# A convolution-attention hybrid on one core: causal attention by transposed scores, with six images in one schedule

## What is computed

```python
# 1. attention over channels: 8 heads of 24 channels, 24x24 logits per head
x = x + w_proj @ (softmax(norm(q) @ norm(k).T * temperature) @ v) + b_proj
# 2. causal attention over tokens: 6 heads of 32, 1024 x 1024 scores per head
t = layer_norm(tokens(x)); q, k, v = t @ Wq, t @ Wk, t @ Wv
att = softmax(where(causal, q @ k.T / sqrt(192), -inf)); x = x + att @ v
# 3. feed-forward, binarized weights, activations quantized by the
#    largest magnitude over a group of 6 images (5 groups, the last 2 images give 0)
x = x + quant(gelu(quant(layer_norm(x) @ sign(W1).T + b1)) @ sign(W2).T + b2)
```

## Time and profile before

| | |
|---|---|
| median of three executions | 4890.53 us |
| profiled execution, its span | 4894.14 us, 4892.3 us |
| TensorE busy (matmul), mean granted clock | 4119.3 us (84%), 0.948 |
| VectorE busy | 3418.6 us (70%) |
| ScalarE busy | 2759.7 us (56%) |
| GpSimd busy | 359.1 us (7%) |
| DMA, mean of 16 engines | 13.3% |

### The profile page before, as it was taken

How to read it: one execution, slowest core, us unless ns; L and a number is a source line. 1 busy time by engine, 2 the same in 40 slices (tenths; PEclk the granted TensorE clock), 3 DMA queues, 4 the chain that set the end, 5 groups by cost and what they waited for, 6 DMA issues and landing times.

```text
span 4892.3 us, 114220 instructions
## 1 busy us (share of the span) xinstructions
PE 4119.3 (84%) x38848; PEld 2965.8 (61%) x38848; DVE 3418.6 (70%) x6624; ACT 2759.7 (56%) x5791; POOL 359.1 (7%) x311
## 2 busy tenths in 40 slices
PE   3989897879898878989887879889878989887878
PEld 2766664566676636766664566666536667664565
DVE  3767677777676667767677777676677767676776
ACT  1555555646565555555555655555565555565655
POOL 0000002000000120000002000000120000002000
PEclk8999998999999989999998999999989999998999
DMA  2111111011121101111111011121101111111011
GB/s 60 40 34 34 34 40 27 0 47 34 34 54 40 34 0 39 34 34 34 35 40 27 0 47 34 41 53 34 34 0 40 34 34 34 40 34 27 0 40 40
DMA packets 46377, 161.59 MB, mean 33 GB/s; under 512 B 10098, under 2 KB 10612, under 8 KB 45684
## 3 DMA queue, kind: packets, MB, share of 16 engines
q1 hardware_dynamic: 45812, 154.38, 13.3%
HBM read 28.52 MB, written 25.17 MB: 11 GB/s over the span
## 4 chain that ended last, share of the span: by engine, by line
issue 76%; PE 13%; POOL 6%; DVE 2%; ACT 2%; DMA 0%; POOLq 0%; SPq 0%; ACTq 0%; DVEq 0%
PE S L685 5%; PE PT L754 4%; POOL hi_z L478 2%; POOL hi_z L497 1%; POOL rstd L473 1%; POOL rstd L493 1%; ACT work L908 1%; POOL NK L468 1%; PE PT L649 1%; PE OUT L669 1%; DVE work L364 0%; DVE nmax L1103 0%; DMA B<-in_b 0%; PE S L635 0%; PE S L693 0%
## 5 line engine op out<-in xcount | busy, mean ns | idle before, releaser
L863 ACT ACTIVATE work<-S,nmax 128x256 f32<-128x256 f32 (+7 forms) x1536 | 1141.4, 744 | 1113.6 <-DVE nmax L1103 1048.5
L1103 DVE TENSOR_REDUCE nmax<-S 128x1 f32<-128x256 f32 (+7 forms) x1536 | 1157.4, 754 | 845.8 <-PE S L637 830.0
L649 PE MATMUL PT<-ident,work 128*128 128x128 f32 x6912 | 1112.7, 281 | 214.2 <-DVE work L364 184.4
L649 PEld LDWEIGHTS PT<-ident,work 128*128 128x128 f32 x6912 | 748.0, 142 | 430.5 <-DVE work L364 260.4
L364 DVE COPY work<-PT 128x512 f32<-128x512 f32 (+3 forms) x1536 | 893.5, 583 | 57.4 <-PE PT L649 52.3
L685 PE MATMUL S<-odd,W1b 128*128 (+1 forms) x2160 | 567.2, 419 | 96.0 <-ACT work L908 47.0
L685 PEld LDWEIGHTS S<-odd,W1b 128*128 128x128 f16 x2160 | 215.2, 106 | 419.8 <-issue 148.6
L635 PE MATMUL S<-KS,QS 128*128 128x512 f16 (+3 forms) x1152 | 333.1, 345 | 105.7 <-issue 57.0
L867 ACT ACTIVATE work<-PT 128x512 f32<-128x512 f32 (+3 forms) x768 | 331.8, 432 | 53.4 <-PE PT L649 53.4
L637 PE MATMUL S<-causal,identb 128*128 128x128 bf16 x1536 | 342.4, 223 | 0.0
L635 PE MATMUL S<-odd 128*128 128x512 f16 (+3 forms) x1152 | 315.1, 328 | 16.9 <-ACT work L863 14.8
(11 more groups left out here) (183 smaller groups left out, 5760.9 us busy)
## 6 DMA issues: line engine op xcount, KB each, us to landing
X<-in_x SPq DMA_DIRECT2D x32, 768.0 KB, 5.4
odd<-hi_z SPq DMA_DIRECT2D x128, 192.0 KB, 4.3
odd<-odd SPq DMA_DIRECT2D x128, 192.0 KB, 4.3
out_y<-work SPq DMA_DIRECT2D x64, 384.0 KB, 3.7
QS<-hi_z SPq DMA_DIRECT2D x64, 192.0 KB, 3.7
QS<-odd SPq DMA_DIRECT2D x64, 192.0 KB, 4.2
KS<-hi_z SPq DMA_DIRECT2D x64, 192.0 KB, 4.7
KS<-odd SPq DMA_DIRECT2D x64, 192.0 KB, 4.6
```

The source lines that it names most:

```text
L649: last = tr(bank[:, P * (j - c0):P * (j - c0) + P], PS[m % 2][:, m // 2 % 2, P * j:P * j + P], ident[:, :])
L863: A(PS[n % 2][:, n // 2 % 2, 0:w], S[:, n % 2, 0:w], ACT.Exp, bias=nmax[:, n % MAXES:n % MAXES + 1], accum_out=rowsum[:, sum_col(n):sum_co ...
L1103: v.tensor_reduce(nmax[:, n % MAXES:n % MAXES + 1], S[:, n % 2, 0:P * (qtile(n) + 1)], AX.X, ALU.max, negate=True).then_inc(max_made, 1)
```

## The change

Attention no longer turns the exponentials. It makes the scores twice.

A first pass (`score_block`, `max_block`) makes them with queries on partitions, as before, only to take the row maxima: 72 blocks of up to 512 keys an image, in two banks (`SM`). `split_rows` cuts the negated maxima into three bfloat16 parts, `turn_rows` turns them with matmuls, and ScalarE copies them into `MR`, where a row belongs to a head and a part.

A second pass (`turned_block`) makes them with keys on partitions: 72 blocks of 128 keys by up to 512 queries, in three banks (`ST`). A second matmul adds the negated maxima to every row (`SEL` picks the head's three rows of `MR`), and a third adds the mask where a block touches the diagonal. ScalarE takes the exponential of a block, without bias and without row sum, into a ring of 12 buffers (`PX`). `weigh` multiplies a set of four (or two) blocks with V, in four groups of 32 array columns, with up to 512 queries moving. GpSimd adds up the blocks of a head (`presum`), 66 instructions an image, and TensorE sums over the keys with 16 matmuls of one column per accumulated group (kind "s"), VectorE takes the reciprocals, and the result of a group is turned back (kind "b") and added (`add_to_t1`).

One image is 72 ticks. The maxima of an image are taken 40 ticks ahead of its turned blocks (`LEAD`). The three rounds of the pair loop become one unrolled stretch of 432 ticks and 8 more; at its end the first 40 maxima blocks of the next group's first image and the front of it are done too. The last two images have a stretch of their own. The front's steps stand at new ticks, from 38 before to 30 behind tick 0 of the image that precedes theirs. The layer norm's normalising moves from VectorE to GpSimd (8 instructions an image), its rounding from VectorE to ScalarE (2). The front has two banks of its own. TensorE waits for all 16 stacking DMAs before the first block of an image. The tail is the same.

```diff
+TICKS = 72
+LEAD = 40
+RING = 12
...
+def make_blocks():
+    out = [(c, h, c, j, h) for c in range(2) for j in range(4 * c + 4) for h in range(4)]
+    out += [(2, h, c, j, h - 4 + 2 * c) for j in range(8) for c in ((1, 0) if j < 4 else (1,)) for h in (4, 5)]
+    return out
...
+def width(i):
+    return 512 - max(0, P * BLOCKS[i][3] - 512 * BLOCKS[i][2])
...
+def pv_tick(k):
+    return set_blocks(k)[-1] + (5 if SETS[k][1] == 0 else 3)
...
+    for hs, c in (((0, 1, 2, 3), 0), ((0, 1, 2, 3), 1), ((4, 5), 1), ((4, 5), 0)):
+        for h in hs:
+            for qt in range(4 * c, 4 * c + 4):
...
+ROWS = [(0, 0), (0, 1), (1, 1), (1, 0)]
+ROWS_DONE = [15, 47, 63, 71]
+ROWS_AT = [17, 49, 65, 71]
...
+SLOTS = {"xt0": -38, "xt1": -36, "xt2": -34, "xt3": -32, "g0a": -30, "g0": -29, "g1a": -27, "g1": -26, "wg0": -24,
+         "wg1": -22, "na": -20, "rb": -15, "u": -9, "mt": -6, "t0": 0, "t1": 1, "t2": 2, "t3": 3, "z0": 12, "z1": 13,
+         "z2": 14, "z3": 15, "qk0": 16, "qk1": 17, "qk2": 18, "qk3": 19, "qk4": 20, "qk5": 21, "v0": 24, "v1": 26,
+         "v2": 28, "v3": 30}
+SMALL_SLOTS = {"norms": -19, "nk": -18.5, "rdiag": -17, "logits": -14, "xexp": -13, "attn": -11, "ln_stats0": 2,
+               "ln_stats1": 4, "rstd": 4.5, "ln_norm0": 5, "ln_norm1": 6, "ln_round0": 7, "ln_round1": 8, "lo0": 8.5,
+               "lo1": 9}
...
-        T0 = sb("T0", [P, 2, TT, C])
+        T0 = sb("T0", [P, TT, C])
...
-        PT = [ctx.enter_context(nc.psum_tensor(f"PT{i}", [P, 512], F32)) for i in range(2)]
+        S4 = ctx.enter_context(nc.psum_tensor("S4", [P, 512], F32))
         OUT = ctx.enter_context(nc.psum_tensor("OUT", [P, 512], F32))
-        FR = ctx.enter_context(nc.psum_tensor("FR", [P, 512], F32))
-        FB = [FR[:, :], S[:, 0, 512:1024]]
+        FRONT = [ctx.enter_context(nc.psum_tensor(f"FR{i}", [P, 512], F32)) for i in range(2)]
+        FB = [FRONT[0][:, :], FRONT[1][:, :]]
+        SM = [S[:, 0, 0:512], S[:, 0, 512:1024]]
+        ST = [S[:, 1, 0:512], S[:, 1, 512:1024], S4[:, :]]
+        PT = [S4, FRONT[1]]
...
+                    for t in range(4 * int(name[-1]), 4 * int(name[-1]) + 4):
+                        pool.tensor_scalar(Z[:, t, :], t_of(u)[:, t, :], mv[:, t, 0:1], rstd[:, t:t + 1], ALU.subtract,
+                                           ALU.mult).then_inc(norm_made, 1)
...
+            def presum(g, images, x):
+                u, i = divmod(x, TICKS)
+                grp, h, c, j, hh = BLOCKS[i]
+                if not sums_of(i):
+                    return
+                w = width(i)
+                pool.wait_ge(exp_made, after(g, 0, TICKS, x + 1))
...
+                b = before_in_acc(i) if j else None
+                acc, new = ACC[hh][:, 512 - w:512], PX[x % RING][:, 0:w]
+                if j == 0:
+                    alone(pool)
+                    o = pool.tensor_copy(ACC[hh][:, 0:P], PX[x % RING][:, 0:P])
+                elif j == 1:
+                    o = pool.tensor_tensor(acc, PX[(TICKS * u + b) % RING][:, 512 - w:512], new, ALU.add)
+                else:
+                    pool.wait_ge(summed, after(g, u, SUMMED[-1], SUMMED[b]))
+                    o = pool.tensor_tensor(acc, acc, new, ALU.add)
+                o.then_inc(summed, 1)
...
+            def score_block(g, x):
+                u, i = divmod(x, TICKS)
+                h, qt, k0, w, last = MAXES[i]
+                n = sm_of_max(x)
+                if i == 0:
+                    for st in stacked:
+                        pe.wait_ge(st, after(g, u, STACKS, STACKS))
+                if n >= 2:
+                    pe.wait_ge(sm_free[n % 2], after(g, 0, SM_PER // 2, n // 2))
+                o = mm(SM[n % 2][:, 0:w], QS[u % 2][:, h, P * qt:P * qt + P], KS[u % 2][:, h, k0:k0 + w], start=True,
+                       stop=not last)
+                if last:
+                    o = mm(SM[n % 2][:, w - P:w], identb[:, :], causal[:, :], start=False, stop=True)
+                o.then_inc(scores_full, 1)
...
+            def turned_block(g, images, i, x):
+                u, b = divmod(x, TICKS)
+                grp, h, c, j, hh = BLOCKS[b]
+                w, hg = width(b), h // 4
+                n = sm_of_rows(u, ROWS.index((hg, c)))
+                pe.wait_ge(sm_free[n % 2], after(g, 0, SM_PER // 2, n // 2 + 1))
+                wait_bank(pe, g, images, i)
+                q0, bank = 512 * c + 512 - w, ST[i % 3]
+                diag = w < 512 or j == 4 * c
+                mm(bank[:, 0:w], KS[u % 2][:, h, P * j:P * j + P], QS[u % 2][:, h, q0:q0 + w], start=True, stop=False)
+                o = mm(bank[:, 0:w], SEL[hg][:, h - 4 * hg, :], MR[hg][:, q0:q0 + w], start=False, stop=not diag)
+                if diag:
+                    o = mm(bank[:, 0:P], causal[:, :], identb[:, :], start=False, stop=True)
+                o.then_inc(ring_full, 1)
+            def weigh(g, u, k):
+                grp, j = SETS[k]
+                blocks = set_blocks(k)
+                pe.wait_ge(exp_made, after(g, u, TICKS, blocks[-1] + 1))
...
+                for b in blocks:
+                    _, h, c, _, hh = BLOCKS[b]
+                    w = width(b)
+                    o = mm(OUT[32 * hh:32 * hh + 32, 512 - w:512], V[u % 2][:, j, D * h:D * h + D],
+                           PX[(TICKS * u + b) % RING][:, 0:w], start=(j == 0), stop=(j == 4 * c + 3),
+                           tile_position=(0, 32 * hh))
+                o.then_inc(pv_made, 1)
+            def attention(g, images, first, last):
+                ends = spans(images)
+                for e in range(first, last):
+                    for i, _, x in entries_at(e, images, "x"):
+                        turned_block(g, images, i, x)
+                    x = e + LEAD
+                    if x < ends["max"]:
+                        score_block(g, x)
+                    for u in range(images):
+                        for k in range(len(SETS)):
+                            if TICKS * u + pv_tick(k) == e:
+                                weigh(g, u, k)
+                    for i, kind, n in entries_at(e, images, "sb"):
+                        wait_bank(pe, g, images, i)
+                        if kind == "s":
+                            pe.wait_ge(summed, after(g, n // 3, SUMMED[-1], SUMMED[LAST_OF[n % 3]]))
+                            for q in range(4):
+                                for hh in range(4):
+                                    o = mm(ST[i % 3][:, 4 * q + hh:4 * q + hh + 1], ACC[hh][:, P * q:P * q + P], ones[:, 0:1],
+                                           start=True, stop=True)
+                        else:
+                            pe.wait_ge(oT_made, after(g, 0, 3, n + 1))
+                            for q in range(4):
+                                o = tr(ST[i % 3][:, P * q:P * q + P], oT[:, P * q:P * q + P], ident[:, :])
+                        o.then_inc(ring_full, 1)
+                    fronts_at(e, lambda name, u: front_part(name, g, u), SLOTS.items(), 1, ends["front"])
+                    if x < ends["max"]:
+                        for u, k in rows_at(x):
+                            turn_rows(g, u, k)
+            attention(0, GS, -LEAD, 0)
...
+                        w = width(x % TICKS)
+                        act.wait_ge(ring_full, after(g, 0, RING_PER, i + 1))
+                        if x >= RING:
+                            u, b = divmod(x - RING, TICKS)
+                            act.wait_ge(pv_made, after(g, u, len(SETS), SET_OF[b] + 1))
+                            act.wait_ge(summed, after(g, u, SUMMED[-1], SUMMED[reader(b)]))
+                        A(PX[x % RING][:, 0:w], ST[i % 3][:, 0:w], ACT.Exp).then_inc(exp_made, 1)
...
+                    for n in range(3 * images):
+                        u, grp = divmod(n, 3)
+                        if e == TICKS * u + LAST_OF[grp] + 4:
...
+                            A(oT, OUT[:, :], ACT.Copy).then_inc(oT_made, 1)
+                    fronts_at(e, lambda name, u: front_part(name, g, u), order, 1, ends["front"])
...
+                            hg, c = ROWS[k]
+                            n, m = sm_of_rows(u, k), 3 * len(HEADS[hg])
+                            act.wait_ge(rows_full, after(g, u, 4, k + 1))
+                            A(MR[hg][0:m, 512 * c:512 * c + 512], SM[n % 2][0:m, :], ACT.Copy).then_inc(sm_free[n % 2], 1)
...
+                dve.wait_ge(scores_full, after(g, 0, TICKS, x + 1))
...
+                v.tensor_reduce(o, SM[n % 2][:, 0:w], AX.X, ALU.max, negate=True).then_inc(sm_free[n % 2], 1)
...
+                v.tensor_tensor(fin.rearrange("p (h d) -> p h d", h=16), ST[i % 3].rearrange("p (h d) -> p h d", h=16),
+                                rsums[:, :].unsqueeze(2).broadcast_to([P, 16, D]), ALU.mult).then_inc(t1_step, 1)
+                dve.wait_ge(t1_step, after(g, 0, 6, 2 * n + 1))
+                f = fin.rearrange("p (i e) -> p i e", i=4) if grp < 2 else fin.rearrange("p (i c e) -> p i c e", i=4, c=2)
```

(13 more changed lines are left out.)

534 lines of the change are left out of this document (271 added, 263 removed).

## The result

The changed kernel takes **5754.06 us** (5748.66 to 5766.7) against 4889.48 us (4886.1 to 4891.87) for the one before, run beside it: a ratio of **1.1773, 95% interval 1.1751 to 1.1794**. The forecast was 5245 us and 4880 to 5500 us: the sign was right, the size was not. The profiled execution has a span of 5764.9 us.

A forecast was written before the change was run, and what follows sets the result against it. A ring of scores, maximum, exponential, transpose and copy binds, TensorE close behind. An image: 103.2 work + 6 + 5.7 stalls + 4 clock + 1 small waits = 120 us; 1647 + 30 x 120 gives 5245 us, range 4880 to 5500.

The forecast's parts named there:

- its term for the clock: TensorE's clock falls to half behind idle stretches, twice an image: 4 us an image, 0 to 8 as ends.
- All three have room in 103 us on the average: Per image VectorE has about 60 us of work, ScalarE and GpSimd some 65 each, so all fit within TensorE's 103.
- the break-even: Whole kernel: groups of six images plus an unchanged tail of about 260 us; faster only under about 108 us an image.
- My line, 1647 + 30 x image: Whole span from the time of one image, start and last two images included; about 5247 us at 120 us an image.
- TensorE's work, 103.2 us: TensorE's matmuls for one image after the change: 71.4 us for attention, the rest the front; 103.2 us in all.
- that rival: In the product with V, four blocks don't run together: 13.5 us more an image, 5650 us; chance 0.05.
- The other engines: VectorE, ScalarE and GpSimd loads per image; a GpSimd addition of 512 columns 1.13 us, GpSimd busy about 2100 us in all.
- Stall one: Tick 12: TensorE's z waits for GpSimd's layer-norm chain, about 6 us an image, 4 and 8 as ends.
- Stall two: Tick 32: the next image's maxima wait for all sixteen DMAs, 5.7 us an image, 3 and 7 as ends.
- the fourth: Rival: clock low over most of an image, or GpSimd slower while VectorE works; 5490 to 5850 us; chance 0.13.

The follow-up runs named there:

- fillers: Changed kernel plus 14 and 20 unneeded matmuls of 512 columns in the stalls of ticks 9 and 11; 5704.06 us, ratio 1.1648.
- the small-sums run of the last order: Later-order kernel with 16-bit row sums and the softmax mask added from the score bank, GpSimd's sums cut to 8 elements (row sums not computed); 4882.4 us, ratio 0.9975.
- the score-bank addition: Changed kernel with VectorE multiplying in place in the score bank, so addition L1284 reads one operand there; 5727.47 us, ratio 1.1692.
- the mask run: Later-order kernel with 16-bit row sums, and the softmax's block-mask addition reading its first operand from the score memory; 5166.1 us, ratio 1.057.

## Why the prediction was right in sign and wrong in size

Two steps of the prediction failed. The first is its term for the clock, 4 us an image with 0 to 8 as ends: it let the clock fall behind idle stretches only, and by the estimate below 12.7 us are lost. The second is the overlap in "All three have room in 103 us on the average", which let VectorE and GpSimd work beside each other without a price; GpSimd's additions turned out to cost 9.5 us an image. The time of an image in us, split in three, for the kernels that bear on this, from the distances of the first exponentials of neighbouring images (25 images inside the groups; for the kernel before, from a group's first exponential to its last, divided by six):

| | image | TensorE idle | lost at the low clock | the rest, work |
|---|---|---|---|---|
| kernel before | 109.0 | 11.4 | 1.9 | 95.7 |
| forecast | 120 | 12.7 | 4 | 103.2 |
| changed kernel | 136.1 | 19.4 | 12.7 | 104.0 |
| GpSimd's sums at 8 elements | 127.1 | 11.2 | 11.9 | 103.9 |
| one row-sum matmul a set | 123.1 | 21.5 | 6.0 | 95.7 |
| row sums from a 16-bit copy | 121.5 | 20.1 | 4.9 | 96.5 |
| fillers | 134.1 | 12.9 | 9.8 | 111.4 |

Idle is the time without a recorded matmul (6 + 5.7 + 1 in the forecast); lost is half of the time in which TensorE is busy at 1.2 GHz, an estimate. Of the 16.1 us that were missing, idle time is 6.7, the clock 8.7 and work 0.8. GpSimd's additions make idle time and hardly touch the clock; the lumps of row sums make work and low clock and no idle time.

- **What bounds, and the break-even.** "The change pays if its image takes less than about 108 us": the small-sums run of the last order has images of 108.6 us and lies 0.25% under the kernel before (row sums left out). The groups and tails were placed right. My line, 1647 + 30 x image, gives 5730 us for 136.1. The other 35 are the ends: the last two images take 222.3 us, not 186 (they have the longer images too), and the first exponential starts at 172.3, 6 us later than I had it.
- **TensorE's work, 103.2 us.** Held. V with four blocks beside each other: eight records of 512 columns in 1.07 us in tick 56, the second four 0.45 us behind the first, so that rival is out. Row-sum records are 0.112 us apart. The gap of 131 ns for 512 columns, from the Trainium skill, "TensorE: Matmul & The Clock Gate", section Back-to-back issue gap, was not seen: they start 0.216 us apart.
- **The other engines.** GpSimd was to be busy some 2100 us and is 2456.3. Its additions take 1.27 us for 512 columns (1.13 taken). The sentence "All three have room in 103 us on the average" counted each engine by itself. VectorE's L1284 and its like lose time to GpSimd's additions. A rule that I had left out bears on this. The Trainium skill, "SBUF — State Buffer", section "SBUF: two separate sides", says that a GpSimd instruction and a VectorE instruction with two inputs in SBUF (if GpSimd's reads SBUF too), or in a mode that uses two ports, exclude each other for a whole instruction. The trace agrees: 0.69 us alone, up to 5.76 us beside five additions, and 0.69 again with one operand in the score memory. It is worse than the rule as I read it, since the wait lasted through a train of five.
- **Stall one.** "So it stands about 6 us", at z. The normalisation is 1.03 us, outside my bounds of 0.2 to 0.55, which came from a subtraction's rate; eight cost 8.2 us instead of 3.0. And the place was wrong: z starts 1.2 us behind the matmul ahead of it, 0.6 of it idle. In tick 11 TensorE has distances of 3.2 us ahead of block 11 (1.6 to 9.2) and 5.1 behind it (means of 25 images). I had costed the chain to its end, and left out what is queued on ScalarE behind its roundings: exponentials and the copy of the maxima.
- **Stall two.** 5.7 us forecast. Distances of 2.13 us for the transfers (tick 32) and 2.36 for the split of the last row maxima (tick 31). The first was too large, the second was not in the sum.
- **Not seen at all.** 3.1 us an image idle in tick 57, by L1284, up to 4.5 in one; it went with the small sums, and with the score-bank addition rb's wait took its place.
- **Clock.** The term that was most mis-sized: 4 us, with 0 to 8 as ends, against 12.7. I had it fall behind idle time alone, twice an image. It falls also at 90 of 96 lumps of row sums, and those that were shorter or gone took most of these falls with them (18 and 1 of 96). The one-row-sum run and the 16-bit run gave 4 and 5 us an image more than the matmuls (and the addition) they took away. What of a lump calls for the lower clock is not shown: the two runs changed its length, its weights and the columns it moves together. Nor is it settled whether each of the 12.7 us is one that the image would gain; the fillers show 1.7 us returned, 7.4 of work more against 6.5 of idle time and 2.9 of clock less.
- **The rivals.** What came about is the fourth, "the clock stays low over most of an image [...] or GpSimd is slower than its row while VectorE works", 128 to 140 us an image, to which I gave 0.13. Its time came about, its mechanism only in part. The clock is low for 31 to 38 us of an image, not over most of it, though the row sums that it names do have a part. Its second half was the wrong way round: GpSimd's additions of 512 columns take 1.25 to 1.29 us nine times in ten, whatever VectorE does, and VectorE is slowed. Against it I had set the clock of 0.96 to 0.98 before; but that stream had only one lump of one-column matmuls an image, 16 records in 1.5 us (L558 in the earlier trace rows), and at one of 32 does the clock fall: no evidence on lumps of 32 records in 3.6 us.

## What to carry to other kernels

Before work goes to an idle GpSimd, list VectorE's operations with two operands (or one and its result) in the main memory that will run beside it: each can stand for as long as GpSimd has instructions in a row. Read the operand from the score memory or give the operation to ScalarE, all of them at once, since a single one only hands its wait to the next. Price matmuls with one moving column by their weights and by the clock behind them, and give them 16-bit weights if they can have them (16 of them held TensorE for 0.41 us instead of 3.49). When a step is given to another engine, follow what queues behind its consumer, not only the chain itself.

## What the runs showed that I had not expected

- Lumps of matmuls that load 128 columns of weights and move one column, recorded as 100% busy for 3.6 us, are followed by the lower of the two clocks with no hole between, 90 times in 96. The first lump of an image (from 1522.5 us) sees it already before its end, at 1525.0. With 16-bit weights (0.41 us a set) and the score-bank addition six stretches at half the clock became three.
- GpSimd normalises 192 elements a partition in 1.03 us, even at 91 us, where nothing runs beside it, but adds 256 in 0.73 us.
- VectorE's addition with both operands in the main memory waited through five GpSimd instructions, 5.76 us. The normalisation, with one tensor operand, got its turn after each (0.93 to 1.05 us). That is no rule for one operand: the scaling L1237, also one tensor in and one out, lasted 3.77 us in the mask run beside five additions in a row, 0.26 alone. What decides is not shown.
- A reciprocal costs VectorE 3.36 us for 512 elements and 0.26 for 16.
- 7.3 us of useless matmuls an image made the kernel 50 us faster.
